# Weighing in four parts between the projections, and the output's norming behind two rotary products

## The reference, cut to what matters

```
def attn_layer(x, Wqkv, qs, ksc, Wo):
    q, k, v = jnp.split(x @ Wqkv, 3, -1)              # 16 heads of 64
    q = l2norm(q) * qs ; k = l2norm(k) * ksc
    q = q * cos * scale + rotate_half(q) * sin * scale
    k = k * cos * inv   + rotate_half(k) * sin * inv
    out = local_attention(q, k, v)                    # windows of 32, looking back one window
    return out @ Wo
def ffn_layer(x, g, bln, W1, b1, W2, b2):
    xn = layer norm of x; a, gate = split(xn @ W1 + b1)
    return a * gelu(gate) @ W2 + b2
for i in range(6):
    x = attn_layer(shift_tokens(x), ...) + x
    x = ffn_layer(shift_tokens(x), ...) + x
```

## Time and profile before

| | |
|---|---|
| median of 3 runs | 4473.97 us (4472.48 to 4486.27) |
| the profiled execution's own time | 4476.09 us |
| its span, first to last instruction | 4474.3 us |
| mean granted TensorE clock | 0.957 of full speed |
| TensorE busy with products | 4011.1 us (90%) |
| VectorE / ScalarE / GpSimd busy | 3350.9 / 2549.0 / 2263.7 us |

### The profile page before, as it was taken

One profiled execution on the slowest core, in us unless ns is written; L12 is line 12 of the kernel. 1 busy time (PEld: TensorE's weight loads), 2 busy tenths in 40 slices (PEclk: granted clock), 3 DMA queues, 4 the chain that ended last, 5 costly groups with the idle time before them and its releaser, 6 DMA issues. The chain is left out here.

```text
span 4474.3 us, 176762 instructions
## 1 busy us (share of the span) xinstructions
PE 4011.1 (90%) x69459; PEld 2733.0 (61%) x69459; DVE 3350.9 (75%) x6660; ACT 2549.0 (57%) x5258; POOL 2263.7 (51%) x3052
## 2 busy tenths in 40 slices
PE   7999549677999999999999999999999999999995
PEld 5777326564666666666666666666666666666663
DVE  4767341677888887888788887888878888888884
ACT  4777434123566665666566665666656666656662
POOL 0000000104766666666566666666666666667661
PEclk9999669798999999999999999999999999999998
DMA  1000004002222222222222222222222222222221
GB/s 43 5 5 3 1 22 103 7 0 63 66 57 61 62 79 61 62 57 61 71 69 62 58 63 73 66 61 58 61 74 66 62 57 65 75 64 60 60 60 28
DMA packets 457941, 238.77 MB, mean 53 GB/s; under 512 B 42374, under 2 KB 448340, under 8 KB 457172
## 3 DMA queue, kind: packets, MB, share of 16 engines
q1 hardware_dynamic: 457172, 228.08, 19.6%
HBM read 32.92 MB, written 2.10 MB: 8 GB/s over the span
## 5 line engine op out<-in xcount | busy, mean ns | idle before, releaser
L2006 POOL TENSOR_TENSOR n_pre<-n_tt 128x512 f32<-128x512 f32 x768 | 967.8, 1278 | 851.8 <-DVE n_tt L2503 830.8
L2503 DVE TENSOR_TENSOR n_tt<-n_pp,n_rot 128x1024 f32<-128x1024 f32 x768 | 921.1, 1219 | 114.2 <-ACT n_sq L2356 105.0
L2101 PE MATMUL n_pp<-n_wqkv,XS 128*128 128x512 f32 x1536 | 787.4, 613 | 10.0 <-DVE n_tt L2503 7.4
L2042 POOL TENSOR_TENSOR n_nq<-n_pre,n_rn 128x512 f32<-128x512 f32 x768 | 777.7, 1045 | 31.1 <-POOL n_rn L2029 24.3
L2356 ACT ACTIVATE n_sq<-n_pp 128x512 f32<-128x512 f32 x768 | 459.8, 599 | 534.3 <-PE n_pp L2101 530.9
L2368 ACT COPY n_qkT<-n_pp 128x512 f32<-128x512 f32 x768 | 432.8, 593 | 243.8 <-PE n_pp L2113 241.3
L2113 PEld LDWEIGHTS n_pp<-ident,n_nq 128*128 128x128 f32 x3072 | 355.6, 141 | 204.4 <-issue 168.7
L2512 DVE TENSOR_REDUCE n_ss<-n_sq 128x16 f32<-128x1024 f32 x384 | 466.3, 1214 | 5.8
L2113 PE MATMUL n_pp<-ident,n_nq 128*128 128x128 f32 x3072 | 440.8, 275 | 27.0 <-DVE XS L2583 16.6
L2125 PEld LDWEIGHTS n_pp<-n_OT,n_wo 128*128 128x128 f32 x3072 | 357.4, 191 | 153.3 <-ACT n_OT L2374 151.6
L2519 DVE TENSOR_REDUCE n_nm<-n_pS 128x8 f32<-128x512 f32 x384 | 246.7, 684 | 198.7 <-PE n_pS L2147 198.6
(11 more groups left out here) (261 smaller groups left out, 7029.9 us busy)
## 6 DMA issues: line engine op xcount, KB each, us to landing
n_V<-n_Vn SPq DMA_DIRECT2D x768, 128.0 KB, 2.4
n_Vx<-n_Vn SPq DMA_DIRECT2D x384, 128.0 KB, 2.4
n_Vx<-n_Vn SPq DMA_DIRECT2D x576, 64.0 KB, 2.1
n_wqkv<-in_L_ffn_Wqkv SPq DMA_DIRECT2D x36, 256.0 KB, 2.9
e_w<-in_L_ffn_w SPq DMA_DIRECT2D x32, 256.0 KB, 2.9
m_Y<-e_ye SPq DMA_DIRECT2D x64, 64.0 KB, 2.1
n_wo<-in_L_ffn_Wo SPq DMA_DIRECT2D x6, 512.0 KB, 4.1
a_xs<-in_L_attn_x SPq DMA_DIRECT2D x16, 128.0 KB, 2.1
```

The costliest lines, as they stand in the source:

```text
L2006: nc.gpsimd.tensor_tensor(d, s[0], s[1][:, :, ::-1, :], ALU.add).then_inc(s_add, 1)
L2042: nc.gpsimd.tensor_tensor(nq[:, r, :].rearrange("p (h d) -> p h d", d=D), d, bcast(rn[:, j, t, 8 * half:8 * half + 8], 2, D), ALU.mult).th ...
L2101: nc.tensor.matmul(pp[:, c % 2, :], XS[:, b, j * P:(j + 1) * P], wqkv[:, t * I + 512 * half:t * I + 512 * half + 512], start=True, stop=Tr ...
L2503: nc.vector.tensor_tensor(tt[:, c, :, :].rearrange("p s (h d) -> p s h d", d=D), bcast(pp[:, c % 2, :].rearrange("p (h d) -> p h d", d=D), ...
```

## The change

`weigh` gets a parameter, the column blocks that it computes. In each visit but the first its four blocks are now four calls, each followed by one full-array product: block 0, `project(0)`, block 1, `project(1)`, block 2, `project_v(0)`, block 3, then (where b is even and j = 0) `hidden(Q, 2)`, then `project_v(1)`. The weighing in `ending` stays whole. ScalarE takes `gelu(Q, 2)` behind the first two squares. VectorE takes `norm_output` (and behind it `gated(Q, 2)`) after the first two rotary products, not before them, and also after `make_shift`. No instruction is added or left out, no wait is added.

```
-            def weigh(u, j):
-                for c in range(4):
+            def weigh(u, j, chunks=range(4)):
+                for c in chunks:
...
                 if back:
                     weights_ready(l * NG + eb // 2, g - 1, eb % 2, ej)
                     held(pe, s_held)
-                    weigh(eb % 2, ej)
-                if ff and b % 2 == 0 and j == 0:
-                    hidden(Q, 2, g - 1)
+                    weigh(eb % 2, ej, range(0, 1))
                 project(0)
+                if back:
+                    weigh(eb % 2, ej, range(1, 2))
                 project(1)
+                if back:
+                    weigh(eb % 2, ej, range(2, 3))
                 if b + 1 < NB or not last:
                     if (b, j) == (NB - 1, 0):
                         pe.wait_ge(s_wv, 32 * (l + 2))
-                    for half in range(2):
-                        project_v((b + 1) % NB, j, half, bank("v", b + 1, j, half))
+                    project_v((b + 1) % NB, j, 0, bank("v", b + 1, j, 0))
+                if back:
+                    weigh(eb % 2, ej, range(3, 4))
+                if ff and b % 2 == 0 and j == 0:
+                    hidden(Q, 2, g - 1)
+                if b + 1 < NB or not last:
+                    project_v((b + 1) % NB, j, 1, bank("v", b + 1, j, 1))
...
-                if ff and b % 2 == 0 and j == 0:
-                    gelu(Q, 2)
                 if proj:
                     square(tile, 0)
                     square(tile, 1)
+                if ff and b % 2 == 0 and j == 0:
+                    gelu(Q, 2)
...
-                if back:
-                    norm_output(g - 1, ej)
-                if ff and b % 2 == 0 and j == 0:
-                    gated(Q, 2)
                 if (qb, qj) == (NB, 0) and not last:
                     after(dve, s_t, 4 * tile)
                     tables(l + 1)
@@
                 if proj:
                     rotate(tile, qj, 0)
                     rotate(tile, qj, 1)
+                if back:
+                    norm_output(g - 1, ej)
+                if ff and b % 2 == 0 and j == 0:
+                    gated(Q, 2)
                 maxima(g, j)
```

## The result

The changed kernel takes 4610.78 us, the median of 4 runs (4610.12 to 4624.61); the kernel before, run beside it, 4479.89 us (4472.48 to 4486.27, 4 runs). The ratio is 1.030, 95% interval 1.028 to 1.032: slower, by 135 us where the forecast had 98.

What follows compares the result with a forecast made beforehand. The prediction took TensorE, busy 90% of the span, to set the network's pace. Sum: 4476 + 130 + 15 + 30 + 38 - 93 - 22 = 4574 us, 4572 against the median, +2.2%; range 4490 to 4650.

Steps and rivals of the forecast that it cites:

- the prediction's own signs of being wrong: Stops still in the weighing's quarters, more than 40 us of them in the scores, or masks at 5.4 us or less.
- rival 3: Worse: late loads move into the scores and quarters keep the later ones' slower pace; 4719 us, one alone 4649 or 4609; chance 0.12.
- Changes of form, +130: Split weighing on TensorE: three more changes each way between small form and full array, +0.68 us a visit, 191 weighings.
- Rival 1: Faster: changes of form cost half, as a projection's weight load overlaps a short stretch's drain; 4453 us; chance 0.09.
- Late loads, -93 + 15: TensorE's late program loads: 93 us of stops in the weighing go, 15 us are added in the scores.
- rival 4: The stops are not loads but something of the values' placement, and stay; 4674 us; chance 0.06.
- project(1), +30: TensorE's earlier project(1) waits 0.65 us for the previous visit's fourth rotary product in 47 visits: 30 us.
- The working's 1.81 us: Predicted distance of project(1) behind the start of the weighing, before 2.37 us.
- turn_output, +38: Where b is odd, j = 0, turn_output waits for VectorE's later norming: 0.8 us in 47 visits, 38 us.
- hidden(2), 0: hidden(2) moves nearer the masks that overwrite its tile; gated(2), 0.75 us, just fits: 0, to +10.
- The clock, -22: Half-speed stretches of TensorE follow the weighing's stops, so most of 33 us lost goes with them: -22 us.

Runs made afterwards that it cites:

- the experiment with one mask product: Kernel before, first of eight mask products put between the two value projections in 143 visits: 4521.95 us, ratio 1.0100.
- both orders of VectorE mended: Changed kernel with rotary product 3 ahead of the statistics and make_shift behind rotary product 0: 4561.50 us, ratio 1.0165 to the kernel before.
- The halves: Weighing in two halves, not four parts, every visit: 4497.36 us, ratio 1.0074 to the kernel before; with rotary product 3 ahead of the statistics 4461.71 us, 0.9976.
- the pair that differs by 126 increments: Kernel before with dummy TensorE increments, 768 instructions between weighings: 6032.37 us; the same with 126 more in the first visit: 5867.28 us.
- the quartered placements: Kernel before, each placement of values moving only a quarter of its elements, TensorE's instructions the same: 4473.16 us, ratio 1.0014.
- product 3 first: Changed kernel with rotary product 3 ahead of the statistics on VectorE where b is even, j = 1: 4549.90 us, ratio 1.0187 to the kernel before.
- the stop at `make_shift` is moved: Changed kernel with rotary product 0 ahead of make_shift where b is odd, j = 0: 4584.63 us, ratio 1.0238 to the kernel before.
- the three kernels with VectorE's order mended: Changed kernel with rotary product 3 ahead of the statistics, with make_shift behind rotary product 0, or with both: ratios 1.0187, 1.0238, 1.0165 to the kernel before.

## Why the prediction was right, and which term was not

The sum said slower by 2.2%, it is 3.0% (2.8 to 3.2), inside the range; the mechanisms were the right ones. One of the prediction's own signs of being wrong came true all the same: it had put it at more than 40 us of stops in the scores, and there are 45.9. That is half of rival 3, late loads that move into the scores; for that half alone the prediction had given 4609 us, and 4610.78 were measured; that the numbers meet is chance, as other terms were off too.

- *Changes of form, +130.* As sized, by the timeline: a quarter takes 0.58 us with its changes against 0.57, the masks come at 5.76 against 5.7, and the experiment with one mask product gives 0.31 us for a way in and out against 0.33. Rival 1, half of that price, is out. By the Trainium skill a change of tiling mode drains the engine ("TensorEngine Tiling (Array Packing)", key properties); that it has a price agrees with the 45 us for 143 more ways in and out.
- *Late loads, -93 + 15.* This is the term that was mis-sized. The weighing's part went as predicted (93.0 to 6.4). In the scores I added 15 us and it was 36.4, and 10.5 more came in the turning behind them, which I had not thought of: net 40 us gained, not 78. With both orders of VectorE mended, too, 69.9 us stay. The prediction had the reason, that a quarter of a weighing stands before the scores where four products stood, and took its low side. The halves, with two products there, have 22.8 and 29.6 us in the scores, between 9.5 (four products) and 45.9 (one), which speaks for it; it was not isolated from the other shifts.
- *Nature of the stops.* Loads of 256 instructions: that they hang on places 256 apart is shown by the pair that differs by 126 increments, and that these are loads by the packet ahead of each stop; rival 4 fell with the quartered placements. The Trainium skill calls the crossing of such a boundary "mostly hidden" ("Runtime: NRT & Kernel Launch", instruction fetch mechanics); this agrees with the kernel whose boundary falls at 122 of each weighing (3 stops, 7 us) and not with the one at 248 (161 stops, 217 us).
- *project(1), +30.* It was 44.2 us, 0.96 in the mean of 46 visits (2.6 us in all before). I had taken 0.65, between 0.5 and 0.9 of the two visits in the earlier trace rows; the first of them was the typical one. The working's 1.81 us should be 1.82 by its own terms, which changes nothing. The cause is shown: with product 3 first the wait goes.
- *turn_output, +38.* 22.9 us as a wait for the norming; 28 us in time when the stop at `make_shift` is moved. Both waits together are worth 61 us where the forecast had 68. The stop at `make_shift` (62.9 us in 47 visits) is as the working had it; what I did not see is that `rstd` waits behind product 3's addition on GpSimd, so that one move of VectorE shortens both waits.
- *hidden(2), 0.* The masks wait 3.4 + 1.4 us at most. It just fits, as written.
- *The clock, -22.* The traces show 5 us at most: 44.4 us of the network at half speed in place of 54.6. I had taken it that the slow stretches go with the stops of the weighing, but stretches at half speed remain where those stops are gone. The other three executions of the changed kernel had a granted clock of 0.961 to 0.964 over the whole run, the profiled one 0.959, so outside the trace it may have been more.

By these, with the waits as in the traces (project(1) less the 2.6 us of before), 130 - 40 + 42 + 23 - 5 = 150 us, against 148.5 between the two traces and 135 between the medians. The forecast's 98 differs from this by four errors: it put the gain of the loads 38 too high, the gain of the clock 17 too high and `project(1)` 12 too low, against 15 too much for `turn_output`. That 150 meets 148.5 so closely is partly luck, since the same working is some 20 us high for the three kernels with VectorE's order mended.

## What to carry to other kernels

Where TensorE runs a dense stretch of small products, look whether its unexplained stops keep one distance modulo 256 in its own instruction order; if they do, interleave long products only in the stretches in which the boundary falls late, since a way into the small form and out again cost 0.3 us in every visit here, stop or no stop. When an operation is moved earlier on one engine, list what it waits for from the visit before: 0.56 us earlier made a wait of 44 us in all. A new order on another engine can be harmless only because of the move it came with, so try each alone before one is kept.

## What was not expected of the hardware

- Stops at program boundaries depend sharply on where the boundary falls: in the kernel before those in the weighings are all at instruction 156 or later of 256; at 122 in every weighing 3 stops are left, at 248 there are 161.
- Increments of a semaphore on TensorE stand 0.151 us apart though each is busy for 0.051: some 87 a visit brought about 1400 us, or 7 us a visit.
- Half clock follows a stop at one place (0.51 in the earlier trace rows, inside a weighing) and not at another (1.00 behind the stop at 2834.29, inside the scores), after nearly the same pause, 2.06 and 2.22 us.
